# Dilation and depthwise convolution on one core: two VectorE row parts in turn, two-row projections begun ahead, and the first blocks loaded during the statistics

## What is computed

```python
x = x + dilation(group_norm(x), kernel)            # 11 x 11 taps: max over (pixel - k[tap]), padded with -1e30
out = einsum('oi,bihw->bohw', proj_w, gn(x)) + proj_b   # 1 x 1 projection over the 32 channels
h = conv(out, dw_w, 3 x 3, padding 1, per channel) + dw_b
h = batch_norm(h); h = gelu(h)
x = x + bilinear_resample(gn(x), offsets from h)
```

## Time and profile before

| what | us |
|---|---|
| median of 3 runs | 10605.95 (10602.75 to 10606.29) |
| the profiled execution, its time | 10607.43 |
| its span, first to last instruction | 10605.6 |
| statistics | 0 to 182 |
| of it, VectorE's instructions on the tiles (L237) | 12.0 to 168.9 |
| dilation | 182 to 8805 |
| convolution | 8805 to 9744 |
| resample | 9744 to 10606 |
| one addition of POOL in the convolution (L953, L959) | 4.54 |

### The profile page before, as it was taken

One profiled execution on the slowest core, in us unless ns is written; L12 is line 12 of the kernel. 1 busy time (PEld: TensorE's weight loads), 2 busy tenths in 40 slices (PEclk: granted clock), 3 DMA queues, 4 the chain that ended last, 5 costly groups with the idle time before them and its releaser, 6 DMA issues. The chain is left out here.

```text
span 10605.6 us, 74703 instructions
## 1 busy us (share of the span) xinstructions
PE 8667.4 (82%) x18080; PEld 3370.3 (32%) x18080; DVE 10072.2 (95%) x5621; ACT 9214.2 (87%) x6867; POOL 9428.6 (89%) x3274
## 2 busy tenths in 40 slices
PE   1888888888888888888888888888888887887888
PEld 0333333333333333333333333333333333333333
DVE  7999999999999999999999999999999998998999
ACT  1999999999999999999999999999999996776666
POOL 2999999999999999999999999999999995666988
PEclk9999999999999999999999999999999998998999
DMA  8787878787878787788888878888878874443666
GB/s 308 150 161 150 160 149 158 151 156 153 157 152 156 154 157 154 152 157 157 156 157 155 157 154 157 156 157 155 157 154 157 156 138 141 159 158 157 254 250 251
DMA packets 442850, 1757.44 MB, mean 166 GB/s; under 512 B 23968, under 2 KB 130464, under 8 KB 392864
## 3 DMA queue, kind: packets, MB, share of 16 engines
q0 software_dynamic: 278528, 1110.51, 59.1%
q1 hardware_dynamic: 163872, 642.05, 16.0%
HBM read 397.22 MB, written 201.33 MB: 56 GB/s over the span
## 5 line engine op out<-in xcount | busy, mean ns | idle before, releaser
L545 PE MATMUL chain<-dx,mats 128*128 128x512 f32 x10240 | 5013.9, 635 | 974.5 <-ACT chain L595 972.9
L483 POOL TENSOR_TENSOR m<-m,u 128x2048 f32<-128x2048 f32 x1024 | 4779.6, 4828 | 23.2 <-ACT m L577 22.9
L679 DVE SCALAR_TENSOR_TENSOR acc_a<-m,kt,acc_a 128x2048 f32<-128x2048 f32 x1344 | 3163.0, 2353 | 68.9 <-POOL m L479 19.7
L545 PEld LDWEIGHTS chain<-dx,mats 128*128 128x128 f32 x10240 | 1928.2, 198 | 4060.1 <-ACT chain L595 2130.4
L595 ACT ACTIVATE chain<-chain,gap_r 128x1024 f32<-128x1024 f32 x2560 | 2700.0, 1089 | 246.4 <-PE chain L545 243.6
L679 DVE SCALAR_TENSOR_TENSOR acc_a<-t,kt,acc_a 128x2048 f32<-128x2048 f32 x1024 | 2412.0, 2355 | 34.2
L454 POOL DMA_DIRECT2D t<-u x1024 | 1612.7, 1686 | 437.0 <-ACT t L577 376.7
L479 POOL TENSOR_TENSOR m<-u,m 128x2048 f32<-128x2048 f32 x384 | 1888.7, 4919 | 0.0
L577 ACT ACTIVATE t<-dx,gap_l 128x2048 f32<-128x2048 f32 x768 | 1541.8, 2008 | 0.0
L545 PE MATMUL chain<-u,mats 128*128 128x512 f32 x3072 | 1456.0, 605 | 74.5 <-ACT chain L595 74.5
L679 DVE SCALAR_TENSOR_TENSOR acc_a<-u,kt,acc_a 128x2048 f32<-128x2048 f32 x576 | 1357.0, 2356 | 20.5
(11 more groups left out here) (146 smaller groups left out, 6986.0 us busy)
## 6 DMA issues: line engine op xcount, KB each, us to landing
t<-u POOLq DMA_DIRECT2D x1024, 1059.0 KB, 8.8
u<-x_dram SPq DMA_DIRECT2D x32, 2688.0 KB, 25.5
xw<-x_scratch SPq DMA_DIRECT2D x65, 1152.0 KB, 7.3
hw<-h_scratch SPq DMA_DIRECT2D x66, 1024.0 KB, 9.3
xt<-x_dram SPq DMA_DIRECT2D x32, 2048.0 KB, 14.4
x_scratch<-x SPq DMA_DIRECT2D x64, 1024.0 KB, 11.0
h_scratch<-h SPq DMA_DIRECT2D x32, 2048.0 KB, 7.3
out_dram<-res SPq DMA_DIRECT2D x64, 1024.0 KB, 4.9
```

The source lines that it names most:

```text
L483: nc.gpsimd.tensor_tensor(m[j % MP], m[j % MP], rows, ALU.add).then_inc(m_ready, 1)
L545: added = nc.tensor.matmul(chain[h][:, r:r + 2, :], weight, src[:, top:top + 2, dj:dj + W], start=False, stop=True, skip_group_check=True)
L679: nc.vector.scalar_tensor_tensor(out=acc_a[:], in0=src, scalar=k_base, in1=acc_a[:], op0=ALU.subtract, op1=ALU.max).then_inc(a_done, 1)
```

## The change

In the statistics and the dilation: the buffers `u`, `dx`, `outside` and the semaphores of the loads and differences are made in `build`, outside both stages. DVE sets their pads at the head of the statistics; SP issues the loads of the first two windows behind the last of its tiles; POOL makes the seven pieces of the first window's differences within the statistics block.

In the convolution: the projection has ten pieces, of 1, 2, ..., 2, 1 rows, one matmul each; `pp` holds two rows, and there are three buffers `hp`. PE's and ACT's orders begin pieces 0 to 3 of the next window within this one. DVE takes the steps of two parts in turn.

```diff
 def build(...)
+            u = [windows.enter_context(nc.sbuf_tensor(f"u{s}", [P, UR, UC], F32)) for s in range(2)]
+            dx = [windows.enter_context(nc.sbuf_tensor(f"dx{s}", [P, UR, UC], F32)) for s in range(2)]
+            outside = windows.enter_context(nc.sbuf_tensor("outside", [P, R, W], F32))
...
 def stats_and_tables(...)
@@ SP, behind the loads of xt
+                sp.wait_ge(pads_set, 1)
+                load_window(nc, sp, x_pl, u, outside, win_loaded, 0, 0, 0, top=True)
+                load_window(nc, sp, x_pl, u, outside, win_loaded, 1, 1, 0)
+            @block.gpsimd
+            def _(pool):
+                pool.wait_ge(pads_set, 1)
+                pool.wait_ge(win_loaded[0], 32)
+                for piece in FIRST_PIECES:
+                    difference(nc, u, dx, dx_ready, 0, piece)
@@ DVE, ahead of the first memset
+                for s in range(2):
+                    nc.vector.memset(u[s][:, :, 0:R], NEG)
+                    nc.vector.memset(u[s][:, :, R + W:UC], NEG)
+                    nc.vector.memset(dx[s][:, :, UC - 1:UC], 0.0)
+                nc.vector.memset(outside[:], NEG).then_inc(pads_set, 1)
...
 def dilation(...)
@@ SP
-                sp.wait_ge(pads_set, 1)
-                load_window(0, 0, 0, top=True)
-                load_window(1, 1, 0)
                 copy_shared(1, 1, 0)
@@ POOL
                 pool.wait_ge(pads_set, 1)
-                pool.wait_ge(win_loaded[0], loads_done(0, 0))
-                for piece in FIRST_PIECES:
-                    difference(0, piece)
@@ DVE
-                for s in range(2):
-                    nc.vector.memset(u[s][:, :, 0:R], NEG)
-                    nc.vector.memset(u[s][:, :, R + W:UC], NEG)
-                    nc.vector.memset(dx[s][:, :, UC - 1:UC], 0.0)
...
-                nc.vector.memset(outside[:], NEG)
...
 def convolution(...)
-    rows_of = [(0, 1)] + [(1 + q * QR, 1 + (q + 1) * QR) for q in range(PARTS)] + [(HR - 1, HR)]
+    rows_of = [(0, 1)] + [(lo, lo + 2) for lo in range(1, HR - 1, 2)] + [(HR - 1, HR)]
+    AHEAD = 4
+    HP = ((0, 1, 2, 0), (1, 2, 0, 1))
...
+        dve_order = [(0, 0), (0, 1), (0, 2)]
+        for q in range(1, PARTS):
+            dve_order += [(q, 0), (q - 1, 3), (q, 1), (q - 1, 4), (q, 2)]
+        dve_order += [(PARTS - 1, 3), (PARTS - 1, 4)]
...
@@ PE
                 def taps(n, s, q):
-                    pe.wait_ge(evacuated, n * NPROJ + (NPROJ + q + 3))
-                    pe.wait_ge(h_chain, n * DVE_STEPS + (DVE_STEPS + 1 + (q - 1) * CHAIN))
+                    part = hp[HP[s][q]]
+                    pe.wait_ge(evacuated, n * NPROJ + (NPROJ + rows_there(q * QR + QR + 1)))
+                    pe.wait_ge(h_chain, hp_free(n, s, q))
...
+                def window(n, s, g, loads, ahead_g):
+                    for q in range(PARTS):
+                        for e in (AHEAD + 2 * q - 2, AHEAD + 2 * q - 1):
+                            if AHEAD <= e < NPROJ:
+                                project(n, s, g, e)
+                        if q == PARTS - 1 and ahead_g is not None:
+                            pe.wait_ge(xs_loaded[1 - s], loads)
+                            project(n + 1, 1 - s, ahead_g, 0)
+                            project(n + 1, 1 - s, ahead_g, 1)
+                        taps(n, s, q)
+                    if ahead_g is not None:
+                        for e in range(2, AHEAD):
+                            project(n + 1, 1 - s, ahead_g, e)
...
@@ ACT
+                def window(n, s, ahead):
+                    evacuate(n, s, 4)
+                    evacuate(n, s, 5)
+                    tap(n, s, 0, 0)
+                    evacuate(n, s, 6)
+                    evacuate(n, s, 7)
+                    tap(n, s, 0, 1)
+                    evacuate(n, s, 8)
+                    evacuate(n, s, 9)
+                    sum_before(n, s, 0)
+                    if ahead:
+                        evacuate(n + 1, 1 - s, 0)
+                        evacuate(n + 1, 1 - s, 1)
+                    tap(n, s, 1, 0)
+                    tap(n, s, 1, 1)
+                    if ahead:
+                        evacuate(n + 1, 1 - s, 2)
+                        evacuate(n + 1, 1 - s, 3)
+                    sum_before(n, s, 1)
...
@@ DVE
-                        for q in range(PARTS):
-                            dve.wait_ge(taps_ready, n * PARTS + (q + 1))
-                            for step_no in range(CHAIN):
+                        for q, step_no in dve_order:
...
+                            if step_no == 0:
+                                dve.wait_ge(taps_ready, n * PARTS + (q + 1))
+                            else:
+                                dve.wait_ge(h_chain, part_done(n, q, step_no - 1))
...
```

More of the change, by code:

```diff
@@ L150, in build, with load_window, difference @@
     return nc
+FIRST_PIECES = ((0, 4), (4, 8), (8, 12), (12, 16), (16, 20), (20, 24), (24, UR))
+NEXT_PIECES = ((10, 14), (14, 18), (18, 22), (22, UR))
+def load_window(nc, sp, x_pl, u, outside, win_loaded, slot, w, g, top=False, bottom=False):
+    split = R + WR if bottom else R
+    for lo, hi in ((0, split), (split, UR)):
+        if (top and lo == 0) or (bottom and lo > 0):
+            rows = outside[:]
+        else:
+            rows = x_pl[g * P:(g + 1) * P, bass.ds((w * WR + (lo - R)) * W, (hi - lo) * W)] \
+                .rearrange("p (r w) -> p r w", w=W)
+        sp.dma_start(u[slot][:, lo:hi, R:R + W], rows).then_inc(win_loaded[slot], 16)
+def difference(nc, u, dx, dx_ready, buf, piece):
+    lo, hi = piece
+    nc.gpsimd.tensor_tensor(dx[buf][:, lo:hi, 0:UC - 1], u[buf][:, lo:hi, 1:UC],
+                            u[buf][:, lo:hi, 0:UC - 1], ALU.subtract).then_inc(dx_ready, 1)
 def stats_and_tables(nc, x_pl, params, basis_in, mats_in, mats, par, kt, nkt, gap_r, gap_l,
-                     shift1, eps, small, pair_mean):
+                     shift1, eps, small, pair_mean, u, dx, outside, win_loaded, dx_ready):
     TILE = 4096
@@ L384, in _ @@
             def _(sp):
[L385 to L398, removed]
                 def copy_shared(slot, w, g):
@@ L442, in _ @@
             def _(pool):
[L443 to L446, removed]
                 def add_u(c, s, k, j):
@@ L779, in convolution, with rows_there, part_done, hp_free @@
         ADDS = 2 * HALVES
+        dve_order = [(0, 0), (0, 1), (0, 2)]
+        for q in range(1, PARTS):
+            dve_order += [(q, 0), (q - 1, 3), (q, 1), (q - 1, 4), (q, 2)]
+        dve_order += [(PARTS - 1, 3), (PARTS - 1, 4)]
+        after = {tap: no + 1 for no, tap in enumerate(dve_order)}
+        def rows_there(row):
+            return (row + 1) // 2 + 1
+        def part_done(n, q, step_no):
+            return n * DVE_STEPS + (DVE_STEPS + 1 + after[q, step_no])
+        def hp_free(n, s, q):
+            same = [p for p in range(q) if HP[s][p] == HP[s][q]]
+            if same:
+                return part_done(n, same[-1], CHAIN - 1)
+            before = [p for p in range(PARTS) if HP[1 - s][p] == HP[s][q]]
+            return n * DVE_STEPS + (1 + after[before[-1], CHAIN - 1])
         with nc.Block() as block:
@@ L844, in project @@
                     pe.wait_ge(evacuated, n * NPROJ + (NPROJ + e - 1))
[L845 to L849, removed]
+                    nc.tensor.matmul(pp[e % 2][:, 0:hi - lo, :], wg[:, g, :], xs[s][:, lo:hi, :],
+                                     start=True, stop=True).then_inc(projected, 1)
                 def taps(n, s, q):
-                    pe.wait_ge(evacuated, n * NPROJ + (NPROJ + q + 3))
-                    pe.wait_ge(h_chain, n * DVE_STEPS + (DVE_STEPS + 1 + (q - 1) * CHAIN))
+                    part = hp[HP[s][q]]
+                    pe.wait_ge(evacuated, n * NPROJ + (NPROJ + rows_there(q * QR + QR + 1)))
+                    pe.wait_ge(h_chain, hp_free(n, s, q))
                     for r in range(0, QR, 2):
```

104 lines of the change are left out of this document (48 added, 56 removed).

## The result

The changed kernel takes **10679.61 us** (median of 6 runs, 10674.65 to 10682.39), the one before 10604.45 (6 runs, 10599.72 to 10606.29): **1.007 times as long, interval 1.006 to 1.008**. The forecast was 10672, range 10614 to 10726, with 0.80 for slower. The profiled execution of the changed kernel took 10682.39 us, its span is 10680.6, which is 75.0 more than before.

A forecast was written before the change was run, and what follows sets the result against it. The prediction took DVE's chain plus PE's slow start in each window as the bound. From 10607.4, -16 for the start, +77 for 31 longer periods and +3 at the end gave 10671, rounded up to 10672 us; range 10616 to 10725.

The forecast's parts named there:

- The ring: Convolution: a dependence round through PE and ACT, without DVE, takes 28.8 us a window at full clock.
- The slow clock: Convolution: after PE's idleness, a half-clock stretch on taps 0 and pieces 4 and 5 adds 1.7 us, making 30.5 a period.
- Rival B: Convolution: PE's clock stays full, period 28.8, kernel 10616 us; chance 0.12.
- C: Convolution: two slow PE stretches or a long one in each period, 32.2 us, kernel 10725 us; chance 0.10.
- DVE's part: Convolution: independent steps 1.20 us apart, dependent ones 1.32; 24.5 us a window instead of 26.0, not setting the period.
- the tail: Convolution's end: last window's taps 0 to DVE's last step take 32.6 us, against 29.8 before.
- the head: Convolution's opening: less to project before taps 0, but in two-row turns with ACT; effect nothing.
- the +3: Convolution's end: the term for the last window's longer finish, 3 us added to the kernel.
- The start: Statistics and dilation: ACT begins the dilation at 196.3 instead of 212.8; gain 16 us, bounds 14 and 20.5.
- So the two don't compete: End of statistics: DVE's last tile ends at 168.9, before POOL's first difference at 173.
- So the shift is kept whole: Dilation: behind its opening it stays in step with DVE, so the 16 us gain is kept whole.
- Rival A: Convolution: DVE sets the period, 24.5 us, if the ring is over 4 us shorter; kernel 10481 us; chance 0.07.

The follow-up runs named there:

- rotation_kept_busy: Changed kernel with its three part buffers strictly in turn over all windows and four more unneeded matmuls ahead of taps 0 in each window; 10622.21 us.
- dve_in_order: Changed kernel, but DVE takes each part's five steps one after another again; 10678.85 us, 1.0069 of the kernel before.
- pieces_early_dve_in_order: Changed kernel with PE projecting pieces 4 to 9 one part earlier and DVE taking each part's five steps one after another; 10535.43 us, 0.9935.
- differences_late: Changed kernel, but POOL makes the first window's seven differences at the head of the dilation, loads still early; 10674.94 us, 1.0065.
- start_only: Statistics and dilation of the changed kernel with the convolution of the kernel before; 10590.07 us, 0.9985 of the kernel before.
- pieces_early_rotation: Changed kernel with PE projecting pieces 4 to 9 one part earlier and the three part buffers strictly in turn over all windows; 10477.28 us, 0.9879.

## Why the prediction was right

**The ring: right, link by link.** Forecast and measured: from taps to taps through two pieces and an evacuation 2.90 and 2.92; from taps 2 to the sum 2.31 and 2.28; the sum 3.70 and 3.69; the two short evacuations 1.14 and 1.12; the half-window taps 3.97 and 3.97; the last link 1.56 and 1.50. The one duration without a row, the evacuation of two rows, was put at 0.78 on the line between two others and measured 0.78. The period was 30.77 instead of 30.5.

**The slow clock: right, a little small.** 1.7 forecast, 1.85 by `rotation_kept_busy`. The 1.7 is more than the forecast's rows give: the earlier trace rows give 1.5, and the earlier trace rows (1 - 0.53) x 3 = 1.4. The trace of before has the rest just behind them: from 9245 to 9246 the granted clock is still 0.69, another 0.3 us. That a pause of 3.9 us would cost about the same as one of 2.8 was a guess that came out. The stretch falls on taps 0 and not on the pieces. The sum without it, 28.8 a period, is refuted for this kernel: 31 x 1.85 = 57 us. The Trainium skill, "TensorE: Matmul & The Clock Gate", section "What's actually happening", puts the ramp at under 1% of a typical kernel's span and advises against fitting a particular number of slow matmuls; that it need not be modelled is the forecast's reading. The trace agrees with the figure, 0.5% of the kernel, and still the 57 us are most of the measured difference. Rival B falls: the clock did not stay full, and PE's pause was 3.9 us (forecast 4.4). So does C: there is one slow stretch in a period, and it ends with taps 0.

**DVE's part: right.** Steps that do not depend on each other start 1.20 apart, the others 1.32, in the timeline of the change too. The order is worth nothing there (`dve_in_order`), and 26.1 - 24.37 = 1.7 us a period where DVE is the bound. The 26.1 is from `pieces_early_dve_in_order`, which has no true rotation; but in it DVE waits for PE's taps only 0.7 us in 740 (8850 to 9590 us), so this does not make the difference. The Trainium skill, "VectorE: DVE Perf Modes", section "The DRAIN you can't avoid", adds to the rule that the forecast quoted that an instruction that is not held starts earlier, and the forecast left that out. The 1.20 us between steps of 1.28 agree with the addition. The traces disagree with the same section where it says, from tensor_copy, that leaving out the semaphores between chained operations gains nothing: here a step that waits for the one just before it starts 0.12 us later.

**Both ends of the stage: the tail right, the head not.** From the last taps 0 (9774.20) to DVE's last step (9807.04) are 32.8 us, forecast 32.6. But "nothing" for the head failed: the first taps 0 start 25.7 us after the stage opens, 27.8 before. Half of these 2.1 us is the shorter projecting ahead of them (6.13 instead of 7.16). So of the +3 only about 1 is left.

**The start: right in direction, two steps wrong.** Forecast -16; ACT began 13.5 earlier, and the convolution 10.3.
- "So the two don't compete" failed. The statement looked at the tiles' statistics alone. The small instructions behind them run from 177 on, beside POOL's differences. Four are held up for 1.3 to 1.7 us each and two for 0.9 and 0.3: the block's end moved by 8.3 us, not 3.8, where the given bound was 6. `differences_late` shows it by taking POOL away: 1.88 becomes 0.16. The Trainium skill, "SBUF — State Buffer", section "Who interferes with whom", has the rule: a DVE instruction with two inputs in SBUF, or a copy in a two-port mode, and a GpSimd instruction that reads SBUF shut each other out for a whole instruction. The trace agrees in both directions (SBUF inputs 1.88, PSUM input 0.16). The forecast had no term for it.
- PE's opening took 5.09 instead of the 6.68 of the earlier trace rows, which gave back 1.6.
- "So the shift is kept whole" did not hold in this execution. ACT's square of each chunk in the dilation comes 14.2 us earlier at first, and within the first 14 of 64 chunks the lead shrinks to 10.5, where it mostly stays. But this differs from one execution to the next. Nine of the profiles (the changed kernel, `start_only` and seven others) have the same statistics and dilation, and reach the convolution between 8790.5 and 8795.4 us, 10.3 to 15.2 before the 8805.70 of the kernel before; the changed kernel's own is the latest of them. Of ACT's lead at its first instruction (12.5 to 14.9 us) they lose 3.2 and 3.0 (the changed kernel and `start_only`), 0.7 to 1.3 (six of them) or nothing (`pieces_early_rotation`). By their mean, 12.3, the start is 3.7 us short of the forecast and not 5.7; what decides it in an execution was not tried.

The sum: the start gave 6 us less than forecast, the convolution cost 5 more (85 instead of 80). Both point the same way, so the profiled execution came at 10682.4 instead of 10672; the median lies 3 below it. The mechanism of the larger term, the ring and its slow stretch, is confirmed by the experiments; the smaller one has the right sign and two thirds of its size.

**Rival A: wrong for this kernel, right as a condition.** What the change lacked is one part of distance between projecting a piece and needing it, and a rotation that three buffers can keep. Both together make DVE the bound; either alone does not (about 27.4 in every second window, or 30.73 in all).

## What to carry to other kernels

When an order of work is rewritten for several engines that run strictly in order, follow one dependence round until it returns to its own start, and add it up: here the ring of 28.8 us came out of rows of the kernel before, and neither the busiest engine (24.4 us of work) nor the better order on it mattered until the ring was shorter. A tile needed by the very next step of the producing engine costs a hand-over each time; produce it one step ahead. And if n buffers are meant to turn through a loop's body, its number of uses must be a multiple of n: here the body's eight uses of three buffers left, once the ring was short, a wait of 4 us in every second window.

## What the runs showed of the hardware

- Small DVE instructions, 128x2 elements in SBUF, take up to 1.88 us instead of 0.16 while POOL makes its differences beside them, one piece of POOL each; a tensor_scalar of 128x128 takes 1.73 (`differences_late`). A copy from PSUM is not held up (0.16), nor a memset of 128x2048 (1.76 with POOL and without), nor the batch-norm aggregation (3.62). Work moved onto an idle engine was not free.
- Four matmuls put into a pause of PE, whose results nobody uses, made the kernel 55 us faster (10677.36 to 10622.21), since they kept the clock at 2.4 GHz for what followed (granted clock 1.00 where it had been 0.58). Put behind a wait, the same four made the changed kernel 13 us slower (10679.61 to 10692.27).
